# Causal attention stage of a fused transformer kernel: the preparation of the next batch row is laid out anew over the steps

## The reference

```python
qkv = (x @ Wqkv_w + Wqkv_b).reshape(Bb, Ll, 3, Hh, dd)
scores = jnp.einsum('bhid,bhjd->bhij', q, k) * scale
attn = jax.nn.softmax(scores + causal_mask, axis=-1)
y_softmax = jnp.einsum('bhij,bhjd->bhid', attn, v)
...
state = retention * state + Gamma * hebbian        # hebbian = v_t k_t, step by step in time
y_t = jnp.einsum('bhij,bhj->bhi', W_static + state, q_t)
...
g = jax.nn.gelu(x @ gate_w1 + gate_b1, approximate=False)
alpha = jax.nn.sigmoid(g @ gate_w2 + gate_b2)
y = alpha * y_softmax + (1.0 - alpha) * y_stp
return y @ out_w + out_b
```

## Time and profile before

| what | value |
|---|---|
| median of 3 runs | 1810.72 us (1809.93 to 1811.16) |
| profiled execution, its own time | 1810.67 us |
| its span in the trace | 1809.4 us |
| stage c in the trace | about 935 to 1560 us |
| PE, DVE, ACT, POOL busy over the span | 87%, 71%, 61%, 39% |

### The profile page before, as it was taken

How to read it: one execution, slowest core, us unless ns; L and a number is a source line. 1 busy time by engine, 2 the same in 40 slices (tenths; PEclk the granted TensorE clock), 3 DMA queues, 4 the chain that set the end, 5 groups by cost and what they waited for, 6 DMA issues and landing times. The chain is left out here.

```text
span 1809.4 us, 45598 instructions
## 1 busy us (share of the span) xinstructions
PE 1568.5 (87%) x19728; PEld 1003.6 (55%) x19728; DVE 1285.6 (71%) x2035; ACT 1101.3 (61%) x1642; POOL 698.2 (39%) x500
## 2 busy tenths in 40 slices
PE   4577998999999999999977778878888888899999
PEld 2354666778777778777853323433433332566665
DVE  4665745876787687777768768778778886766564
ACT  3265667777777777786733577677677678433321
POOL 4112301544354255425531555556465555301100
PEclk8798998999999999999996989999999999999999
DMA  7864200000000000000142462164236222000000
GB/s 180 198 181 109 41 5 12 2 2 2 1 2 2 2 2 2 2 2 2 48 110 62 146 155 72 48 187 95 71 116 143 72 71 72 1 7 12 7 12 12
DMA packets 43357, 102.59 MB, mean 57 GB/s; under 512 B 3944, under 2 KB 12288, under 8 KB 41428
## 3 DMA queue, kind: packets, MB, share of 16 engines
q1 hardware_dynamic: 40244, 94.17, 20.2%
q10 hardware_dynamic: 2912, 5.51, 1.8%
HBM read 67.42 MB, written 31.46 MB: 55 GB/s over the span
## 5 line engine op out<-in xcount | busy, mean ns | idle before, releaser
L1450 DVE TENSOR_REDUCE arena<-ring 128x2 f32<-128x1024 f32 (+2 forms) x320 | 342.1, 1111 | 88.8 <-PE ring L1307 63.4
L1550 ACT ACTIVATE arena<-ring 128x1024 f32<-128x1024 f32 (+1 forms) x320 | 291.6, 938 | 129.2 <-PE ring L1336 90.2
L1357 PE MATMUL accs<-arena 128*9 128x512 f32 (+3 forms) x1536 | 174.3, 528 | 2.7 <-ACT arena L1550 2.6
L2514 POOL TENSOR_TENSOR arena<-arena 128x1280 f32<-128x1280 f32 x28 | 65.3, 2332 | 287.0 <-PE accs L2275 231.7
L1329 PE MATMUL ring<-arena 51*128 51x512 bf16 (+3 forms) x768 | 124.4, 342 | 46.6 <-DVE arena L1450 24.9
L1300 PE MATMUL ring<-arena 48*128 48x512 bf16 (+3 forms) x768 | 126.6, 342 | 41.9 <-DVE arena L1450 21.7
L2506 POOL TENSOR_TENSOR arena<-arena 128x512 f32<-128x512 f32 x112 | 141.4, 1292 | 3.0 <-DVE arena L2316 3.0
L292 POOL TENSOR_SCALAR xn<-x,moments,rstd 128x128 f32<-128x128 f32 x80 | 64.4, 814 | 198.2 <-DVE rstd L263 182.6
L2781 ACT ACTIVATE arena<-ring 128x512 f32<-128x512 f32 x80 | 47.8, 598 | 147.2 <-PE ring L2636 142.6
L2499 POOL TENSOR_TENSOR arena<-arena 128x1024 f32<-128x1024 f32 x32 | 86.2, 2694 | 108.2 <-DVE arena L2373 108.2
L2741 DVE TENSOR_TENSOR arena<-arena,ring 128x512 f32<-128x512 f32 x80 | 55.0, 688 | 87.8 <-PE ring L2638 74.2
(11 more groups left out here) (346 smaller groups left out, 4225.8 us busy)
## 6 DMA issues: line engine op xcount, KB each, us to landing
arena<-whole_k SPq DMA_DIRECT2D x32, 512.0 KB, 4.6
arena<-whole_q SPq DMA_DIRECT2D x32, 512.0 KB, 6.2
arena<-c_scratch_q SPq DMA_DIRECT2D x14, 384.0 KB, 10.2
arena<-c_scratch_k SPq DMA_DIRECT2D x14, 384.0 KB, 13.3
a_scratch_k<-arena SPq DMA_DIRECT2D x8, 512.0 KB
c_scratch_k<-arena SPq DMA_DIRECT2D x8, 512.0 KB, 3.8
arena<-a_scratch_q SPq DMA_DIRECT2D x9, 384.0 KB, 7.2
arena<-a_scratch_k SPq DMA_DIRECT2D x9, 384.0 KB, 9.5
```

Source lines behind the costliest of these rows:

```text
L1357: mm = nc.tensor.matmul(acc[ci % 2][32 * h:32 * h + HD + 1, a - c * BANK:BANK], c_values[b % 2][:, j, r * HEADS // 2 + 2 * g + i, :], weig ...
L1450: nc.vector.tensor_reduce(dst, src, AX.X, ALU.max, negate=True).then_inc(c_max_taken.up(item), 1)
L1550: nc.scalar.activation(view(c_probs[wi % 4]), view(ps), ACT.Exp).then_inc(c_weights_made.up(item), 1)
```

## The change

Computation and instructions are the same. The items are in another order, and one is split.

1. stats, log, root, q, k and gate1 stand one step earlier; turn 0, turn 1 and v 1 two steps earlier; v 0 three steps earlier, which is ahead of q. The mid part and the write of the queries come one step earlier; those of the keys, gate2 and alpha stay; the loads (L) stand one step earlier, directly behind the keys' write in SP's queue as before.
2. The copy of the high part was issued with q and k. It is an item of its own now (`high`), one step behind q and two steps behind k (step 18, where k itself stood at 17); the subtraction on POOL (L1669, in the changed file L1677) moves with it.
3. S stands one M later.
4. less moves from step 6 of a row's last unit to step 4, beta from step 8 to step 9.
5. The planner gives the new item a cost; its M move accordingly.

```diff
@@ causal_first_act
+        def act_high(b, side):
+            before = ("q", b) if side == "k" else ("k", b - 1)
+            if before[1] >= 0:
+                ac.wait_ge(c_scratch_there[before[0]], before[1])
+            ac.wait_ge(c_full_made, (side, b))
+            nc.scalar.activation(c_parts[:, 0, :], c_full[:, :], ACT.Copy).then_inc(c_split.up((side, b, "high")), 1)
...
-                if before[1] >= 0:
-                    ac.wait_ge(c_scratch_there[before[0]], before[1])
-                ac.wait_ge(c_full_made, (kind, b))
-                nc.scalar.activation(c_parts[:, 0, :], c_full[:, :], ACT.Copy).then_inc(c_split.up((kind, b, "high")), 1)
+                if b == 0:
+                    act_high(b, kind)
+            elif kind == "high":
+                act_high(*item[1:])
@@ causal_order
-                2: [("stats", b, 0)], 3: [("stats", b, 1)], 4: [("stats", b, 2)], 5: [("stats", b, 3)], 6: [("log", b)],
-                7: [("root", b)], 10: [("turn", b, 0)], 12: [("turn", b, 1)], 13: [("q", b)], 14: [("v", b, 0)],
-                15: [("mid", b, "q")], 16: [("write", b, "q"), ("v", b, 1)], 17: [("k", b)], 18: [("gate1", b)],
-                19: [("mid", b, "k")], 20: [("write", b, "k")], 21: [("gate2", b), *loads(b, 0)],
-                22: [("gate exp", b)], 23: [("alpha", b), *loads(b, 1)]}
+                1: [("stats", b, 0)], 2: [("stats", b, 1)], 3: [("stats", b, 2)], 4: [("stats", b, 3)], 5: [("log", b)],
+                6: [("root", b)], 8: [("turn", b, 0)], 10: [("turn", b, 1)], 11: [("v", b, 0)], 12: [("q", b)],
+                13: [("high", b, "q")], 14: [("v", b, 1), ("mid", b, "q")], 15: [("write", b, "q")], 16: [("k", b)],
+                17: [("gate1", b)], 18: [("high", b, "k")], 19: [("mid", b, "k")],
+                20: [("write", b, "k"), *loads(b, 0)], 21: [("gate2", b)], 22: [("gate exp", b), *loads(b, 1)],
+                23: [("alpha", b)]}
...
-                    rows.insert(2, ("S", *units[u - 1], 0))
+                    rows.insert(3, ("S", *units[u - 1], 0))
...
-                side[end + 6].append(("less", b))
-                side[end + 8].append(("beta", b))
+                side[end + 4].append(("less", b))
+                side[end + 9].append(("beta", b))
@@ pool_program
-                    elif kind in ("q", "k"):
-                        b = item[1]
-                        before = ("q", b) if kind == "k" else ("k", b - 1)
+                    elif kind == "high":
+                        _, b, side = item
+                        before = ("q", b) if side == "k" else ("k", b - 1)
```

More of the change, by code:

```diff
@@ L1499, in act_program @@
                         moe_act(item[1:], ps)
-                    elif kind in ("log", "turn", "q", "k", "mid"):
+                    elif kind in ("log", "turn", "q", "k", "high", "mid"):
                         causal_first_act(item, ps)
@@ L1660, in pool_program @@
                         add_bias(item[1])
-                    elif kind in ("q", "k"):
-                        b = item[1]
-                        before = ("q", b) if kind == "k" else ("k", b - 1)
-                        gp.wait_ge(c_split, (kind, b, "high"))
-                        gp.wait_ge(c_full_made, (kind, b))
+                    elif kind == "high":
+                        _, b, side = item
+                        before = ("q", b) if side == "k" else ("k", b - 1)
+                        gp.wait_ge(c_split, (side, b, "high"))
+                        gp.wait_ge(c_full_made, (side, b))
                         gp.wait_ge(c_split, (*before, "mid"))
@@ L1669, in pool_program @@
                         nc.gpsimd.tensor_tensor(c_rest[:, :], c_full[:, :], c_parts[:, 0, :], ALU.subtract).then_inc(
-                            c_split_pool.up((kind, b, "rest")), 1)
+                            c_split_pool.up((side, b, "rest")), 1)
                     elif kind == "mid":
```

## The result

The changed kernel takes 1827.22 us (median of 4 runs, 1823.70 to 1830.93) beside 1810.94 for the kernel before (4 runs, 1809.93 to 1813.65): a ratio of 1.0088, with a 95% interval of 1.0062 to 1.0114. It is slower by some 16 us, where the prediction had it faster by 8. The profiled execution took 1823.70 us, its span 1822.4.

What follows compares the result with a forecast made beforehand. No engine is full; the ring of three PSUM slots, which PE fills in order, was taken to bound the row. Terms -4.5 - 2.0 - 2.2 - 0.8 - 1.5 + 3.0 = -8.0 took 1810.7 to 1802.7 us; range 1796 to 1811.5.

Steps and rivals of the forecast that it cites:

- The keys' operands: Rows 0 to 2: later keys make the next row's first maxima wait 1.0 a row; +3.0 us (0 to +12).
- rival A: First maxima of rows 1 to 3: the keys land too late and the kernel is slower, 1814.3 or more; chance 0.13.
- S one M later: Eight places gain 0.4 each, the last S of row 3 waits longer; together -2.2 us (+1 to -6).
- the work stays the same, so no duration changes: Whole kernel: a change of order can only remove or add waits; no size given.
- Beta: Wait at beta removed: -4.5 us over rows 0 to 2 (3.0 to 8.4), -2.0 in row 3 (0 to -3.6).
- Row 0: Root ahead of read 0 adds 3.6 at S, the wait at k loses 4.4; -0.8 us (+3.6 to -4.4).
- k, gate1 and S: Rows 0 to 2, with the high part: new order around k gains 0.5 a row; -1.5 us (+3 to -5).

Runs made afterwards that it cites:

- e7: Changed kernel with SP's fetch of column 4 issued behind the keys' write and first loads instead of directly ahead of the write; ratio 1.0108.
- e2: Changed kernel with read 2 ahead of the keys' high part in step 18; ratio 1.0033.
- e4: Kernel before with only S moved one M later; ratio 1.0010.
- e13: Changed kernel with S alone back behind two M, read 2 still behind the keys' high part; ratio 1.0035.
- e10: Changed kernel with read 2 ahead of the keys' high part and S back behind two M; ratio 0.9996.
- e1: Changed kernel with the keys' high part directly behind k again, at step 16; ratio 1.0142.
- e3: Kernel before with only less moved to step 4 and beta to step 9; ratio 0.9972.
- e12: Kernel before with only less moved to step 4, beta still at step 8; ratio 0.9967.
- e14: Kernel before with less at step 4, beta at its old step 8, and row 0's keys' high part behind read 2; ratio 0.9955.
- e8: Kernel before with less at step 4, beta at step 9, and the keys' high part behind read 2 for row 0 alone; ratio 0.9950.
- e15: Changed kernel with read 2 ahead of the keys' high part, S back, root back at step 7 and turn 0 at step 9; ratio 0.9968.
- e11: Changed kernel with read 2 ahead of the keys' high part, S back, and k and gate1 back at steps 17 and 18; ratio 1.0010.
- e6: Kernel before with the preparation's items one to two steps earlier, the high parts still inside q and k; ratio 1.0243.
- e16: Kernel before with less and beta moved, the keys' high part behind read 2 in all rows, and S later; ratio 0.9950.

## Why the prediction was wrong, step by step

- **The keys' operands, +3.0: this term failed, by its size.** It named the place, the chain and the sign, and rival A gave 1814.3 or more. The waits came to 15.4 us, 5.1 a row instead of 1.0. Three of its steps were too small. It put the high part's end at 1198.9; it ended at 1202.4, since gate1's matmuls reached ACT only at 1194.20, 5.9 us behind k, with scale, S and two exponentials behind them. It put the low part's end at 1210.8; it was 1213.8. And it took "1 us or so" for the fetch directly ahead of the write, where the landing took 6.8 instead of 2.4 us. e7 shows 5 us as the fetch. So the load was issued 9.4 us later than before (1221.03 for 1211.60), where the term had 3 to 4. Its slack was too large as well: it took 5.4, but before, the second half of the load had landed at 1220.33 and PE began the first M at 1224.45, which leaves 4.1. And PE came there no sooner than before (ready at 1224.97), where the term had 2 to 3 us sooner. Moving read 2 ahead gives 10 us of the time back (e2).
- **S one M later, -2.2: wrong in sign.** Alone it is +1.8, with 0 inside its interval (e4); in the changed kernel it costs 9.6 us (1.0088 to 1.0035, e13). The term priced S as if all else stood still. With S later the planner has the next row's first M behind step 27, where it also stands in the kernel before, and there it meets the late keys; with S back in this order it would stand behind step 29. In all 185 M move with the edit. With the keys mended (e2 to e10) 6.7 us stay, at a lower clock. How much of this is S and how much the planner's M is not shown.
- **"the work stays the same, so no duration changes": this step failed.** No term of the sum has a price for longer matmuls, and they are 13 of the 19 us in the changed kernel's profile. In rows 1 and 2, PE's busy time for the same matmuls goes from 120.6 (row 1 of e10) to 131.0 us (row 2 of e1).
- **Beta, -4.5 and -2.0: right in sum, wrong in part.** Both together gave -5.1 in the runs (e3); but less alone gives as much (e12), and beta's place beside vT nothing that can be told (e14). In row 3, less ahead of read 6 meets scan 6 as the term said. POOL and DVE in e3, where the scan takes 3.05 instead of 2.29 us:

```profile
1532.11 1.04 POOL L1736 TENSOR_SCALAR arena<-arena 128x1024 f32<-128x1024 f32 x1
...
1532.24 3.05 DVE L1460 TENSOR_TENSOR_SCAN arena<-arena 128x1024 f32<-128x1024 f32 x1 [2.32 <-POOL arena L1711]
```

  The 0.8 is near the 1.0 taken. It agrees with the rule of the Trainium skill, page "SBUF — State Buffer", section "Who interferes with whom", that the prediction cites: less was first, and the scan ended 2.1 us after less did, close to its own 2.29.
- **Row 0, -0.8: right.** S waited 4.17 (forecast 4.6) and the 6.05 at k fell to 1.49 (to 1.66). Each half was tried alone too: the high part behind read 2 in row 0 gives 4.0 (e3 to e8), root back gives 5.1 (e10 to e15, where S had waited 7.37), both with intervals that overlap.
- **k, gate1 and S, -1.5: not contradicted.** e11 gives 2.5 for k and gate1, with intervals that overlap and M that move along. What the term had not seen is that without the split the same steps would cost 44 us (e6).

The two late causes overlap: read 2 ahead gives 10.0 us, S back 9.6, both 16.7. With both, the changed kernel is level with before, and with root back it is at 0.9968, no better than less moved by itself. The best kernels of the study, 0.9950, are the kernel before with less earlier and the keys' high part of row 0 behind read 2 (e8), or with it in all rows and S later (e16).

Where the time lies, by the profiles (from the first M to beta of row 3, us) and by the clock of all runs:

| kernel | PE stands | PE busy | together | mean clock of the runs |
|---|---|---|---|---|
| before | 116.8 | 488.4 | 605.2 | 0.953 to 0.954 |
| changed | 122.6 | 501.8 | 624.4 | 0.947 |
| e2 | 107.6 | 504.3 | 611.9 | 0.944 |
| e13 | 110.3 | 503.7 | 614.0 | 0.949 |
| e10 | 114.0 | 491.7 | 605.7 | 0.952 |
| e15 | 107.0 | 499.0 | 606.0 | 0.952 |
| e3 | 111.8 | 488.0 | 599.8 | 0.954 |
| e8 | 108.6 | 487.7 | 596.3 | 0.956 |

The mends took waits away; in e2, PE stands less than in the kernel before, and it still loses, by longer matmuls. Among the 12 runs of one kernel a clock lower by 0.001 goes with 0.95 us more in e2 and 0.75 in e10 (a line through the runs). An estimate from that: the 0.008 between e2 and e10 are 6 to 7 us, about the 6.7 measured, and the 0.006 between before and the changed kernel some 5 of its 16. That time and clock go together is read from the runs; what sets the clock in each order was not isolated.

## What to carry to other kernels

When an item is split off and moved, look first at what stands behind its parts in every queue they enter. The late copy on ACT showed no cost of its own; the subtraction that waited for it held read 2 on POOL for 6.8 us (1197.86 to 1204.63), and that put a 1 MB fetch close in front of the write that mattered. A large transfer 4 us ahead of an urgent one in the same queue delayed it by 5 us here, one 9 us ahead hardly at all; look at when a transfer lands, not at when it is issued. And test parts of a change of order in the company they ship in: of four parts one was good alone, one neutral alone and costly together, and one only affordable because of another. Where a planner lays out the rest of the order, print what it moved before you price an edit of one line, and set a term aside for the clock.

## What was not expected of the hardware

A single long wait can be followed by a long stretch at the lower clock. Windows of the changed kernel around the wait of 5.41 (mean granted clock is the third number from the right):

```profile
1223.00:1229.00 6.00, 1.97 (x41) 0.95 (x38) 1.40 (x2) 1.62 (x2) 2.40 (x5) 1.00 1.03 173
1229.00:1240.00 11.00, 9.44 (x84) 3.74 (x86) 5.92 (x5) 6.37 (x7) 0.53 (x1) 0.53 1.00 172
1240.00:1246.00 6.00, 4.98 (x58) 1.28 (x50) 5.23 (x5) 4.24 (x5) 5.92 (x3) 1.00 0.41 88
```

PE was busy for 2.0 of the 6 us ahead; then the clock was at 0.53 for 11 us, that is at 1.2 instead of 2.4 GHz nearly all the time, although PE worked 9.4 of the 11. At full clock the 9.44 us at 0.53 would be some 5.0 (an estimate, as if every matmul went with the clock), so the slow stretch cost up to 4.4 us, nearly as much as the wait. The other two waits for c_scratch_k look alike: the clock was low for 10.2 us from 1072.6 and for 6.8 from 1383.2. But such a wait is not the only way there: e2 has none of them, and its clock was low for 10.2 us from 1198.8, where the longest wait is 1.49 us, so taking the waits away did not bring the busy time back. The same order can also differ by itself: rows 1 and 2 of e10 took 146.4 and 151.7 us, at 0.99 and 0.93.
